# Spreading 1/rms over the partitions by two DMAs instead of TensorE transposes, in a four-layer graph network

## What is computed

```
agg = epsilon * x + adjacency @ x
h   = agg @ W1 + b1                       # 128 -> 512
h   = silu(h * rsqrt(mean(h*h) + 1e-6) * rms_weight)
x   = layernorm(x + h @ W2 + b2)          # 512 -> 128
```

## Time and profile before

| | before |
|---|---|
| median of 3 runs | 1133.11 us (1129.41 to 1134.9) |
| the profiled execution's own time | 1131.74 us |
| its span in the trace | 1129.9 us |
| PE busy | 1074.6 us (95% of the span) |
| DVE, ACT, POOL busy | 818.6, 709.2, 613.6 us |
| DMA queue of SP | 23.2% of 16 engines' span |
| first neighbour product, first slot product of stage 2, first work of stage 3 | 29.64, 424.16, 485.30 us |

### The profile page before, as it was taken

One profiled execution on the slowest core, in us unless ns is written; L12 is line 12 of the kernel. 1 busy time (PEld: TensorE's weight loads), 2 busy tenths in 40 slices (PEclk: granted clock), 3 DMA queues, 4 the chain that ended last, 5 costly groups with the idle time before them and its releaser, 6 DMA issues.

```text
span 1129.9 us, 24862 instructions
## 1 busy us (share of the span) xinstructions
PE 1074.6 (95%) x8043; PEld 961.1 (85%) x8043; DVE 818.6 (72%) x2549; ACT 709.2 (63%) x1305; POOL 613.6 (54%) x652
## 2 busy tenths in 40 slices
PE   7899999999999959989999999999999999999875
PEld 6799999999999959967888888888888888888764
DVE  4477787777778733624788787878787878788984
ACT  4445555555555532345677787877777777777765
POOL 1244433434343306634466777777777777777865
PEclk9999999999999989989999999999999999999999
DMA  4112323222322126841211121212121212100001
GB/s 162 57 48 84 94 94 95 84 90 90 95 94 85 57 82 205 249 153 48 60 45 57 48 67 48 66 48 67 48 66 48 67 48 67 48 20 19 20 29 38
DMA packets 64190, 84.45 MB, mean 75 GB/s; under 512 B 6464, under 2 KB 33472, under 8 KB 63808
## 3 DMA queue, kind: packets, MB, share of 16 engines
q1 hardware_dynamic: 64064, 82.86, 23.2%
HBM read 57.14 MB, written 25.69 MB: 73 GB/s over the span
## 4 chain that ended last, share of the span: by engine, by line
PE 89%; DVE 4%; issue 3%; POOL 2%; ACT 1%; DMA 1%; SPq 0%; ACTq 0%; DVEq 0%; POOLq 0%
PE banks L160 18%; PE banks L154 12%; PE banks L155 10%; PE banks L156 10%; PE banks L515 10%; PE banks L774 4%; PE banks L684 3%; PE banks L543 3%; PE banks L608 3%; PE banks L659 2%; PE banks L485 2%; PE banks L637 2%; PE banks L575 1%; PE banks L611 1%; PE banks L613 1%
## 5 line engine op out<-in xcount | busy, mean ns | idle before, releaser
L167 POOL TENSOR_TENSOR rstd<-ve,minus_half 128x4 f32<-128x4 f32 x128 | 131.1, 1025 | 52.5 <-DVE ve L1088 49.1
L167 POOL TENSOR_TENSOR r_rms<-ms,minus_half 128x4 f32<-128x4 f32 x32 | 32.3, 1009 | 223.9 <-DVE ms L1052 223.9
L515 PE MATMUL banks<-w,s 128*128 128x128 f32 x768 | 101.2, 275 | 0.4 <-DVE y L1066 0.4
L515 PEld LDWEIGHTS banks<-w,s 128*128 128x128 f32 x768 | 95.6, 192 | 3.3 <-issue 0.5
L154 PE MATMUL banks<-agg_hi,w_hi 128*128 128x512 f32 x192 | 84.3, 439 | 3.2 <-ACT agg_hi L164 3.0
L1078 DVE BATCH_NORM_STATS2 stats<-y 128x6 f32<-128x128 f32 x384 | 82.6, 276 | 2.2 <-POOL y L1445 2.0
L156 PE MATMUL banks<-agg_hi,w_lo 128*128 128x512 f32 x192 | 76.1, 396 | 0.0
L155 PE MATMUL banks<-agg_lo,w_hi 128*128 128x512 f32 x192 | 76.1, 396 | 0.0
L1420 POOL TENSOR_TENSOR y<-ya,yb 128x512 f32<-128x512 f32 x32 | 41.6, 1299 | 63.2 <-PE banks L724 62.5
L1406 POOL TENSOR_TENSOR x_lo<-x1c,x_hi 128x512 fp32r<-128x512 f32 x32 | 41.2, 1287 | 62.7 <-ACT x_hi L164 62.7
L160 PE MATMUL banks<-at,x_rows 128*128 128x128 f32 x512 | 69.7, 280 | 3.9 <-DVE agg_lo L1040 3.0
(11 more groups left out here) (197 smaller groups left out, 3369.8 us busy)
## 6 DMA issues: line engine op xcount, KB each, us to landing
at<-in_at SPq DMA_DIRECT2D x32, 256.0 KB, 2.9
x_rows<-in_x SPq DMA_DIRECT2D x32, 256.0 KB, 2.9
x_scratch<-x SPq DMA_DIRECT2D x32, 256.0 KB, 3.2
ad<-in_ad SPq DMA_DIRECT2D x32, 256.0 KB, 2.6
x1c<-x_scratch SPq DMA_DIRECT2D x32, 256.0 KB, 2.6
atc<-in_at SPq DMA_DIRECT2D x32, 256.0 KB, 3.0
yh<-yh_scratch SPq DMA_DIRECT2D x64, 128.0 KB, 3.4
out<-out_rows SPq DMA_DIRECT2D x32, 256.0 KB, 2.0
```

The lines of the kernel that those rows point to most:

```text
L167: return nc.gpsimd.tensor_tensor(to[:], base[:], minus_half[:], ALU.pow)
L515: last = pe.matmul(bank[7][:, g, :], s[c][:, g, :], w2[:, c, :], start=(c == 0 and g == 0), stop=(c == H0 - 1), skip_group_check=True)
```

## The change

`spread_rms` goes from TensorE, and with it ACT's copy to `rv`. In its place SP stores `r_rms` (128 partitions x 4 numbers) to a DRAM scratch as [graph][node], a scattered store in runs of one fp32, and, when it has landed, loads the 2 KB row of the group into all 128 partitions as `rv`, in a ring of two. agg_hi and agg_lo get two buffers each. The ring of x grows from 4 to 5, that of the plain adjacency shrinks from 2 to 1. The banks are dealt out anew: gram, square sums and conv1 share bank 5. The turns of all engines are rewritten: gram of a group now runs at the end of the group's own turn, its hidden products 0 and 1 one turn later and 2 and 3 two turns later, conv and transform in smaller pieces between them; a group's down parts and layer norm also come a turn later in part.

```diff
@@ rings and signals
-        X_RING, AT_RING, AD_RING, X1_RING = 4, 2, 2, 2
+        X_RING, AT_RING, AD_RING, X1_RING, RV_RING = 5, 2, 1, 2, 2
+        rms_stored, rv_in = ([sem_of(f"{n}{i}") for i in range(2)] for n in ("rms_stored", "rv_in"))
...
+        rms_dram = nc.dram_tensor("rms_scratch", [GROUPS, G, P], F32, kind="Internal").ap()
...
-        agg, agg_hi, agg_lo = rows("agg"), rows("agg_hi", F32R), rows("agg_lo", F32R)
-        rv = rows("rv")
+        agg = rows("agg")
+        agg_hi, agg_lo = ([rows(f"agg_{n}{i}", F32R) for i in range(2)] for n in ("hi", "lo"))
+        rv = [rows(f"rv{i}") for i in range(RV_RING)]
...
-        stage_tile = [rows(f"stage{i}") for i in range(3)]
+        stage_tile = hn[0:3]
@@ SyncE
+            def store_rms(k):
+                until(sp, "r_rms", k)
+                landed(sp, rv_in, k - 2)
+                sp.dma_start(rms_dram[k].rearrange("g n -> n g"), r_rms[:],
+                             allow_slow_non_contiguous=True).then_inc(rms_stored[k % 2], 16)
+
+            def load_rv(k):
+                landed(sp, rms_stored, k)
+                until(sp, "hn2", k - RV_RING)
+                sp.dma_start(rv[k % RV_RING][:], rms_dram[k].unsqueeze(0).to_broadcast([P, G, P])
+                             ).then_inc(rv_in[k % RV_RING], 16)
...
                     stage(load_x, t + 1)
+                stage(store_rms, t - 1)
+                stage(load_rv, t - 1)
+                stage(load_ad, t + 1 - 12)
                 stage(store_x1, t - 6)
-                stage(load_ad, t + 2 - 11)
@@ TensorE
-            def spread_rms(k):
-                until(pe, "r_rms", k)
-                free(pe, ("hcp", k - 7), ("rv", k - 1))
-                for g in range(G):
-                    last = pe.transpose(bank[4][:, g, :], r_rms[:, g:g + 1].to_broadcast([P, P]), ident[:])
-                last.then_inc(sem["spread"], 1)
...
                 if c == 0:
-                    free(pe, ("hn0", k - 1))
+                    free(pe, ("xh0", k - 9), ("hn0", k - 1))
                 if c == 1:
-                    free(pe, ("prod", k), ("hn1", k - 1))
+                    free(pe, ("xh1", k - 9), ("hn1", k - 1))
                 if c == 2:
-                    free(pe, ("ms", k), ("xh1", k - 9), ("hn2", k - 1))
+                    free(pe, ("hn2", k - 1))
                 if c == 3:
-                    free(pe, ("xh0", k - 9), ("hn3", k - 1))
-                split_product(pe, flat(bank[(5, 0, 1, 3)[c]]), w1_hi[:, c * P:(c + 1) * P],
+                split_product(pe, flat(bank[(3, 0, 2, 6)[c]]), w1_hi[:, c * P:(c + 1) * P],
...
             def conv1(k):
                 until(pe, "x1", k)
-                free(pe, ("rv", k + 6), ("hcp", k - 1))
-                by_graph(pe, bank[4], lambda g: x1[k % X1_RING][:, g, :], lambda g: conv1_w[:]
+                free(pe, ("ms", k + 7), ("prod", k + 7), ("hcp", k - 1))
+                by_graph(pe, bank[5], lambda g: x1[k % X1_RING][:, g, :], lambda g: conv1_w[:]
...
                 stage(neighbours, t)
+                stage(down, t - 4, 3)
+                stage(hidden, t - 2, 3)
+                stage(square_sums, t - 1)
+                stage(hidden, t - 2, 2)
                 stage(conv1, t - 8)
+                stage(transform, t - 10, 1)
+                stage(down, t - 3, 0)
+                stage(hidden, t - 1, 1)
+                stage(transform, t - 10, 0)
+                stage(down, t - 3, 1)
+                stage(x1_t, t - 5)
+                stage(hidden, t - 1, 0)
                 stage(down, t - 3, 2)
-                stage(gram, t - 1)
-                stage(x1_t, t - 5)
-                stage(down, t - 3, 3)
-                stage(transform, t - 10, 0)
-                stage(transform, t - 10, 1)
-                stage(hidden, t - 1, 0)
-                stage(hidden, t - 1, 3)
-                stage(square_sums, t - 1)
-                stage(hidden, t - 1, 1)
-                stage(hidden, t - 1, 2)
-                stage(down, t - 2, 0)
-                stage(spread_rms, t - 1)
-                stage(down, t - 2, 1)
+                stage(gram, t)
@@ ScalarE
-            def spread_rms(k):
-                until(act, "spread", k)
-                until(act, "hn2", k - 1)
-                copy(rv[:], bank[4][:]).then_inc(sem["rv"], 1)
...
-                until(act, "dft1", k - 1)
+                until(act, "dft0", k - 1)
                 nc.scalar.activation(hc[:], hcp[:], ACT.Relu).then_inc(sem["hc"], 1)
...
             for t in range(TURNS1):
-                stage(x1_full, t - 6)
-                stage(silu, t - 2, 0)
-                stage(silu, t - 2, 1)
-                stage(spectrum_of, t - 10, 0)
-                stage(conv1, t - 9)
-                stage(spectrum_of, t - 10, 1)
-                stage(silu, t - 2, 2)
-                stage(silu, t - 2, 3)
+                stage(silu, t - 3, 2)
+                stage(silu, t - 3, 3)
                 stage(full, t)
                 stage(high, t)
-                stage(spread_rms, t - 1)
+                stage(x1_full, t - 6)
+                stage(spectrum_of, t - 10, 1)
+                stage(conv1, t - 9)
+                stage(spectrum_of, t - 10, 0)
+                stage(silu, t - 2, 1)
+                stage(silu, t - 2, 0)
@@ VectorE
-                until(dve, "rv", k)
+                landed(dve, rv_in, k)
...
             for t in range(TURNS1):
+                stage(apply0, t - 5)
                 stage(product, t - 1)
-                stage(apply0, t - 4)
-                stage(residual0, t - 3)
+                stage(normalise, t - 3, 2)
+                stage(residual0, t - 4)
                 stage(mean_square, t - 1)
-                stage(stats0, t - 3)
+                stage(normalise, t - 2, 1)
+                stage(stats0, t - 4)
+                stage(low, t)
+                stage(normalise, t - 2, 0)
+                stage(moments, t - 4, 0, LN_EPS)
+                stage(normalise, t - 2, 3)
+                stage(row_sums, t - 12)
                 stage(conv1_bias, t - 8)
-                stage(low, t)
-                stage(moments, t - 3, 0, LN_EPS)
-                stage(row_sums, t - 11)
-                stage(normalise, t - 1, 1)
-                stage(normalise, t - 1, 0)
-                stage(normalise, t - 1, 3)
-                stage(normalise, t - 1, 2)
```

More of the change, by code:

```diff
@@ L47 @@
 FIRST_STEPS = """
-ae nb agg agg_hi agg_lo gram prod sums ms r_rms spread rv hid0 hid1 hid2 hid3 hn0 hn1 hn2 hn3
+ae nb agg agg_hi agg_lo gram prod sums ms r_rms hid0 hid1 hid2 hid3 hn0 hn1 hn2 hn3
 s0 s1 s2 s3 down0 down1 down2 down xb y0 moments0 r0 x1_rows x1t x1 c1 hcp hc dft0 dft1 xh0 xh1 row_sum
@@ L476, in gram @@
                 until(pe, "agg_lo", k)
-                free(pe, ("hn1", k - 1), ("prod", k - 1))
-                split_product(pe, flat(bank[0]), gram_hi[:], gram_lo[:], flat(agg_hi), flat(agg_lo),
+                free(pe, ("hcp", k - 8), ("ms", k - 1), ("prod", k - 1))
+                split_product(pe, flat(bank[5]), gram_hi[:], gram_lo[:], flat(agg_hi[k % 2]), flat(agg_lo[k % 2]),
                               True, True).then_inc(sem["gram"], 1)
@@ L525, in x1_t @@
                 for g in range(G):
-                    last = pe.transpose(bank[2][:, g, :], x1_rows[:, g, :], ident[:])
+                    last = pe.transpose(bank[1][:, g, :], x1_rows[:, g, :], ident[:])
                 last.then_inc(sem["x1t"], 1)
@@ L537, in transform @@
                 if half == 0:
-                    free(pe, ("hn3", k + 8), ("xh0", k - 1))
+                    free(pe, ("hn0", k + 8), ("xh0", k - 1))
                 else:
-                    free(pe, ("hn2", k + 8), ("ms", k + 8), ("xh1", k - 1))
-                psum = flat(bank[(3, 1)[half]])
+                    free(pe, ("hn1", k + 8), ("xh1", k - 1))
+                psum = flat(bank[(3, 0)[half]])
                 for i in range(2):
@@ L817, in full @@
                 until(act, "sums", k - 1)
-                copy(agg[:], bank[6][:]).then_inc(sem["agg"], 1)
+                copy(agg[:], bank[4][:]).then_inc(sem["agg"], 1)
             def high(k):
                 until(act, "nb", k)
-                until(act, "hid2", k - 1)
-                copy(agg_hi[:], bank[6][:]).then_inc(sem["agg_hi"], 1)
-            def spread_rms(k):
-                until(act, "spread", k)
-                until(act, "hn2", k - 1)
-                copy(rv[:], bank[4][:]).then_inc(sem["rv"], 1)
+                until(act, "hid2", k - 2)
+                until(act, "gram", k - 2)
+                copy(agg_hi[k % 2][:], bank[4][:]).then_inc(sem["agg_hi"], 1)
             def silu(k, c):
@@ L1038, in low @@
                 until(dve, "agg_hi", k)
-                until(dve, "hid2", k - 1)
-                V.tensor_tensor(agg_lo[:], bank[6][:], agg_hi[:].bitcast(F32), ALU.subtract
+                until(dve, "hid2", k - 2)
+                until(dve, "gram", k - 2)
```

(9 more changed lines are left out.)

20 lines of the change are left out of this document (11 added, 9 removed).

## The result

The changed kernel takes 1226.18 us, the median of 4 runs (1224.68 to 1227.89), against 1132.44 for the kernel before in the same comparison: a ratio of 1.0828 [1.0804, 1.0852]. It was forecast faster, at 1120; it is 94 us slower. What happened is the fourth rival, the slow scattered store.

The account below looks back on a forecast made before the run. TensorE's work alone was taken to bound the steady turn of 11.56 us. Spread 14.1, filling -2.7 and draining 6.4 give 17.8, less 4.9 for late row sums: 12.9 saved, 1118.8 profiled, 1120 median; range 1113 to 1131.

Parts of the forecast that it names:

- the fourth rival: Scattered store slow, delaying DVE's first normalise of a group; 1165 if it lands in 8.5 us; chance 1.5 in 10.
- the store's landing, "so 3.7": Scattered r_rms store in stage 1: 1.9 for a 32 KB store plus 1.8 for 28 more packets an engine, 7.0 allowed.
- The upper bound of 15: Store's landing in us, if each of 4 packets took its quarter of 1.9 and 32 packets an engine followed.
- The estimate of 7.4: Store's landing by the Trainium skill's page: 2.0 us fixed plus 5.4 for 512 runs.
- the rival's second part: Store and landing past 7.0 us: each us costs a us a turn, some 30 in all; gain gone at 7.4.
- The spread removed: TensorE in stage 1: 32 spreads of 0.44 us save 14.1, leaving turns of 11.12.
- the three tight releases: PSUM banks 5, 0 and 3 in stage 1: slacks of 0.35, 0.15 and 0.2 us, taken as free of waits.
- Rival 3: A tight release fails on bank 0 or 3: PE waits 0.3 us a turn, time 1130; chance 1.7 in 10.
- The fill: Start of stage 1: turn 4 starts at 57.2 against 59.23, net -2.7 us after work put off and spreads already counted.
- The load of `rv` of "at's shape": Load of rv behind the store: 256 KB in 2 KB rows, landing in 2.9 us.
- The adjacency in one buffer: Late row sums: weights issued 8.6 us after stage 2's first slot, not 1.95; 6.7 less 1.8 slack delays stage 3 by 4.9.
- Rival 2: Late row sums before stage 2 cost little: gain 16 to 18 us, time 1115 to 1117; chance 1.8 in 10.

Follow-up runs that it names:

- contig: The changed kernel with r_rms stored contiguously, 128 runs of 16 bytes, values left in the wrong order so the output is not the reference's; 1123.8 us.
- padded: The changed kernel with its 512 runs of 4 bytes placed 64 bytes apart in DRAM and rv loaded from a row of x; 1124.1 us.
- after: The changed kernel itself, storing 512 runs of 4 bytes side by side, against the kernel before; 1226.2 us, ratio 1.0828.
- strided: The changed kernel with contig's contiguous store, DVE's normalise reading rv with a step of 16 bytes to restore the order; 1134.8 us.
- rows: The changed kernel with one small TensorE transpose of r_rms and an ACT copy, so the store is 4 rows of 512 bytes; 1127.8 us.

## Why the prediction was wrong

The step that failed is **the store's landing, "so 3.7"**. It measured 9.8. I had added up packets at the queue's mean of 0.065. From issue to last packet contig with 8 packets an engine takes 1.02 and padded with 32 takes 1.29, so 24 more cost 0.27, or 0.011 each: the term of 1.8 was too high, and padded lands in 1.9 instead of 3.7. What makes 9.8 is a term that I put at nothing: the 6.2 us between the last packet and the landing, which come when 16 runs lie side by side in 64 bytes. The upper bound of 15 holds 9.8, but its reason, a price for each packet, is wrong as well. The Trainium skill, "DMA: Bandwidth & Descriptors", section "Rules for kernel authors", spoke against this store, and the trace agrees with the rule: 9.8 against 1.4 in contig, where the last dimension is contiguous, though padded, which breaks the rule as well, lands in 1.9. The Trainium skill's floor per packet, in the same page's section "Bandwidth", is measured there on loads issued from GpSimd, and the 2.0 us fixed stand in its section "Anatomy of one DMA — SWDGE (gpsimd) path". The estimate of 7.4 from the two would be the same for after and for padded, which land in 9.8 and 1.9, so the runs decide against it.

**What 9.8 costs** was the rival's second part, "past 7.0 each us costs a turn a us, some 30 in all": 2.8 too much, so 84 us and 1204. It is 1226, by two errors that half cancel. The ring of the chain above gives two turns a lap, so each us costs half a us a turn. And both landings count: the load of `rv` takes 5.2 where the row of `at` gave 2.9. Without the two landings a lap is 29.6 - 12.0 - 4.0 = 13.6, so two turns of 11.20 leave 22.4 - 13.6 = 8.8 for both; 9.9 if the three passes (0.43 for 0.23) and the down part (1.40 for 0.89) ran as in contig. The medians sum to 15.0, so a turn should grow by 2.6 to 3.1. From turn 4 to turn 31, 27 turns, after loses 77.6 against contig, 2.87 a turn. Ahead of that lie 15.6: two stores in the fill, 8.1 and 11.2 us, stand in the chain with nothing to hide them. Behind it 9.0 more go until the first slot. Together they are 102.2, and 101.7 lie between the two spans. The rival's path was not right either: it went over `low` and gram, while TensorE waits for the same normalise earlier in the turn, at the bank of transform half 1 (17 of its 19 waits for a normalise). TensorE's clock has a part in the loss that I can't separate. The windows of after (stretch, its length, then busy us and count of PE, PEld, DVE, ACT and POOL, granted clock, DMA share, GB/s):

```profile
60.00:120.00 60.00, 46.22 (x288) 41.87 (x287) 32.51 (x84) 18.52 (x30) 19.37 (x17) 0.89 0.35 71
120.00:400.00 280.00, 243.12 (x1659) 222.79 (x1659) 174.45 (x460) 114.70 (x197) 92.98 (x82) 0.95 0.41 91
```

The windows of contig:

```profile
60.00:120.00 60.00, 60.00 (x438) 55.92 (x437) 51.67 (x136) 27.61 (x46) 28.85 (x26) 1.00 0.39 106
120.00:360.00 240.00, 239.95 (x1777) 224.35 (x1777) 180.89 (x494) 121.70 (x216) 97.38 (x86) 1.00 0.44 113
```

The granted clock of after is 0.89 and 0.95, means over its two levels of 1.2 and 2.4 GHz; TensorE waits behind a normalise in most turns there, and the passes of 0.43 stand behind such waits. In contig it is busy for 239.95 of 240 us, and the clock is 1.00.

**The other steps** can be judged in contig, which has all of the change but the slow store:
- The spread removed: turns of 11.12 forecast, 11.20 measured; the three tight releases hold, with PE busy all the time. Rival 3 is out.
- The fill: turn 4 at 57.2, measured 57.67. The first slot: 406.4, measured 406.54, so the gain to there, 17.8, is 17.6. Both are partly luck. In the fill `r_rms` and the two DMAs come 1.2 earlier than laid out (44.5 for 45.7), and the work behind them, 3.5 in my sum, takes 4.95, with passes of 0.43. Turn 32 starts at 361.49 in place of 359.1, and the drain behind it takes 45.05 in place of 47.3: two errors of 2.4 and 2.3 that cancel.
- The load of `rv` of "at's shape", 2.9: 4.4 in contig, 3.2 to 3.9 in the kernels with a quick store or none that read x. Mis-sized by 1.5, hidden.
- The adjacency in one buffer: weights 8.6 behind the slot, measured 9.5. But the term "6.7 - 1.8 = 4.9" is 7.5: the slack of 1.8 at the last store doesn't exist. From the weights to stage 3 are 59.19 before and 59.14 in contig, so the whole delay reaches stage 3. Rival 2, that this would be cheap, is out too.
- The sum: 12.9 forecast, 8.8 measured in contig's span (1129.9 to 1121.1): 17.6 - 7.5, and 1.3 between the start of stage 3 and the end that I have no reason for.

So with a quick store in its place, but the values in the wrong order, the change gives 1123.8 for a forecast of 1120; of the versions with a quick store that compute the reference strided takes 1134.8 and rows 1127.8. With the slow store it loses seven times the 12.9 that it was to bring. A chance of 1.5 in 10 was too little for a price that no row of the trace bore on, with bounds of 1.9 and 15 around a limit of 7.0.

## What to carry to other kernels

Before a small DMA goes into the pipeline's ring, look at where its runs fall in DRAM: many short runs side by side are the slow case, and a contiguous layout or one tiny transpose ahead of the store takes it away. Padding the destination does so too for the store, but what reading the padded values back costs was not measured; the contiguous layout cost 11 us for the reordering on DVE. When a term rests on an operation that the trace doesn't show, and its bounds lie on both sides of the slack, measure it alone first, and count the ring in laps: how many turns one lap gives sets what a late us costs. The single buffer in front of the barrier was paid for at the barrier, 7.5 us for weights issued 7.5 later.

## What was not expected of the hardware

- 512 runs of 4 bytes land in 9.8 us side by side (8.1 with nothing beside them, up to 12.0), 4.0 at 8 bytes' distance, 2.7 at 16 and 1.9 at 64.
- Their packets are over 1.3 us after the issue in an idle queue, side by side or not; the difference comes between the last packet and the landing, 6.2 us in after and 0.6 in padded.
- Loads in the same turn suffer from such a store: `at` 5.5 and `x_rows` 5.7, against 2.6 and 2.7 in contig.
- A 256 KB load that reads one 2 KB row for all partitions takes 3.2 to 4.4, where the loads of `at`, 256 KB of different rows, take 2.6 to 3.1 in the same kernels.
- DVE reads a 128x512 fp32 operand with a step of 16 bytes in 1.13 us, contiguous in 0.74.
